# One perceiver block on one core: ternary weights transposed by DMA, rounds 1 and 2 in another order, scores ahead of the weighted sum in odd rounds, and the last codes in halves

## The reference

```python
def xattn(Q, K, Wq_d, W_qk, Wkv_d, Wv_u):          # 16 heads of 32
    C_q, C_kv = Q @ Wq_d, K @ Wkv_d                # 512 -> 64, 512 -> 32
    CqWqk = (C_q @ W_qk).reshape(b, n, 16, 32)
    scores = einsum('bnhl,bkl->bhnk', CqWqk, C_kv) / sqrt(32)
    attn = softmax(scores)
    V_up = (C_kv @ Wv_u).reshape(b, nkv, 16, 32)
    return einsum('bhnk,bkhd->bnhd', attn, V_up).reshape(b, n, 512)
def attn(x, Wqkv, bqkv, Wo, bo):                   # one head of 128
    q, k, v = split(x @ Wqkv + bqkv)
    return softmax(q @ k.T / sqrt(128)) @ v @ Wo + bo
def ffn(x, weight, hadamard):
    xh = x @ hadamard
    s = max(max|xh| over the row, 1e-5) / 7
    xq = clip(round(xh / s), -8, 7) * s            # 4-bit codes
    scale = max(mean|weight| over a row, 1e-5)
    wq = where(weight/scale > .5, 1, where(weight/scale < -.5, -1, 0)) * scale
    return xq @ wq.T
x = x + xattn(layernorm(x), ctx, ...)
x = x + attn(layernorm(x), ...)
x = x + ffn(layernorm(x), weight, hadamard)
```

## Time and profile before

| | |
|---|---|
| median of 3 runs | 314.23 us (314.06 to 314.25) |
| profiled execution | 315.06 us |
| its span | 313.3 us |
| TensorE busy | 299.5 us, 96% |
| VectorE busy | 246.9 us, 79% |
| ScalarE busy | 208.1 us, 66% |
| GpSimd busy | 90.0 us, 29% |
| DMA, share of 16 engines | 26.1% |
| chain that ended last | PE 74%, DVE 11%, ACT 6%, DMA 3% |

### The profile page before, as it was taken

How to read it: one execution, slowest core, us unless ns; L and a number is a source line. 1 busy time by engine, 2 the same in 40 slices (tenths; PEclk the granted TensorE clock), 3 DMA queues, 4 the chain that set the end, 5 groups by cost and what they waited for, 6 DMA issues and landing times.

```text
span 313.3 us, 8324 instructions
## 1 busy us (share of the span) xinstructions
PE 299.5 (96%) x3043; PEld 207.5 (66%) x3058; DVE 246.9 (79%) x530; ACT 208.1 (66%) x587; POOL 90.0 (29%) x130
## 2 busy tenths in 40 slices
PE   7997989999999999999999999999999999999993
PEld 6754857667576766768576766768576866648642
DVE  1689798887879878887879878887879878896366
ACT  2578478768596676768596676768596777784400
POOL 2008304140323324051323324051323324141411
PEclk9999799999999999999999999999999999999998
DMA  7995002051311603041310603051311102000001
GB/s 216 376 363 187 4 8 96 19 189 31 106 49 36 186 1 134 17 157 61 108 43 33 184 0 134 17 173 44 110 43 63 26 0 69 19 35 2 33 0 67
DMA packets 20968, 26.94 MB, mean 86 GB/s; under 512 B 10704, under 2 KB 11472, under 8 KB 20944
## 3 DMA queue, kind: packets, MB, share of 16 engines
q1 hardware_dynamic: 20944, 26.62, 26.1%
HBM read 20.71 MB, written 4.19 MB: 80 GB/s over the span
## 4 chain that ended last, share of the span: by engine, by line
PE 74%; DVE 11%; ACT 6%; DMA 3%; SPq 2%; issue 2%; POOL 0%; DVEq 0%; POOLq 0%
PE ps L1009 10%; PE ps L1074 9%; PE ps L957 7%; PE ps L1132 5%; PE ps L1112 4%; PE ps L1078 4%; PE ps L1162 4%; ACT prob L385 4%; PE ps L967 3%; PE ps L1185 3%; PE ps L1156 3%; DMA bo_row<-bo 3%; PE ps L1046 3%; PE ps L1030 2%; DVE mx L614 2%
## 5 line engine op out<-in xcount | busy, mean ns | idle before, releaser
L385 ACT ACTIVATE prob<-ps,nmx,qk_scale 128x128 f32<-128x128 f32 x240 | 89.8, 469 | 34.9 <-DVE nmx L618 34.9
L1009 PE MATMUL ps<-had_s,x3t 128*128 128x512 f32 x104 | 48.2, 605 | 0.7 <-ACT x3t L379 0.7
L614 DVE TENSOR_REDUCE mx<-ps 128x8 f32<-128x1024 f32 x31 | 37.7, 1217 | 7.0 <-PE ps L1132 7.0
L334 POOL TENSOR_TENSOR qk_scale<-aux,power 128x1 f32<-128x1 f32 x16 | 9.3, 580 | 98.4 <-DVE aux L636 98.4
L623 DVE TENSOR_REDUCE sum_a<-prob 128x8 f32<-128x1024 f32 x30 | 35.8, 1210 | 0.0
L379 ACT ACTIVATE prob_t<-ps 128x512 f32<-128x512 f32 x63 | 34.8, 622 | 0.7 <-PE ps L957 0.3
L1009 PEld LDWEIGHTS ps<-had_s,x3t 128*128 128x128 f32 x104 | 18.6, 190 | 24.5 <-issue 22.7
L957 PE MATMUL ps<-ident,prob 128*128 128x128 f32 x240 | 31.8, 276 | 2.1 <-ACT prob L385 2.1
L957 PEld LDWEIGHTS ps<-ident,prob 128*128 128x128 f32 x240 | 26.6, 141 | 5.5 <-ACT prob L385 4.7
L1074 PE MATMUL ps<-x2t,wqkv_s 128*128 128x128 f32 x224 | 28.6, 281 | 0.4
L1074 PEld LDWEIGHTS ps<-x2t,wqkv_s 128*128 128x128 f32 x224 | 26.1, 192 | 2.2 <-ACT x2t L379 1.3
(11 more groups left out here) (200 smaller groups left out, 577.1 us busy)
## 6 DMA issues: line engine op xcount, KB each, us to landing
ct<-ctx_cols SPq DMA_DIRECT2D x16, 512.0 KB, 4.8
xt<-x_cols SPq DMA_DIRECT2D x16, 256.0 KB, 2.9
xr<-x_rows SPq DMA_DIRECT2D x16, 256.0 KB, 4.2
y<-res SPq DMA_DIRECT2D x15, 256.0 KB, 2.0
had_s<-hadamard SPq DMA_DIRECT2D x1, 1024.0 KB, 7.7
w_rows<-weight SPq DMA_DIRECT2D x1, 1024.0 KB, 10.7
wqkv_s<-wqkv SPq DMA_DIRECT2D x1, 768.0 KB, 8.4
wqk<-w_qk SPq DMA_DIRECT2D x2, 128.0 KB, 4.3
```

What stands on the lines that cost most here:

```text
L385: last = nc.scalar.activation(prob[:, h, :], ps[:, h // 4, (h % 4) * P:(h % 4) * P + P], ACT.Exp, bias=nmx[:, h:h + 1], scale=qk_scale[:])
L614: V.tensor_reduce(mx[:, h], ps[:, 2 * half:2 * half + 2, :].rearrange("p r (c k) -> p (r c) k", c=EC), AX.X, ALU.max).then_inc(done["mx"], 1)
L1009: mm = pe.matmul(ps[:, B4, :], x3t[:, c, :], had_s[:, c, :], start=(c == 0), stop=(c == EC - 1))
```

## The change

1. **Ternary weights.** The 16 transposes on TensorE (L946) and the two copies on ScalarE go. In their place SP's queue issues four DMA transposes of a block of 128 x 512 bf16 each, two in round 1 and two in round 2, these behind the DMAs of the codes of pair 0. TensorE waits for all four before the first integer product.
2. **Rounds 1 and 2.** ScalarE copies the latents of round 1 behind all 16 exponentials. `weight_sizes(3)` moves out of round 0 into round 1. `ternary(1)` stands in front of `second_max` in round 1, `ternary(2)` in round 2 in front of amax. Six more constant products stand in front of `transposed(2)` in round 1, and three more near the start of the program.
3. **Scores first in odd rounds** (from round 3 on): TensorE makes ckv in front of s2, and the scores in front of p2's transpose and the weighted sum. VectorE copies ckv (`context`) in place of ScalarE, has the row variance in front of the q_t copy, and makes both halves of the maxima at the end of the odd round; the next, even, round has none of its own at its start.
4. **The end.** The integers of pair 13 stand in front of the transposes of x2n, with one constant product in place of three. The codes of pair 15 are made, transposed and clipped in two halves of 256 columns.

The diff, cut to its core:

```diff
+        def scores_first(i, par):
+            return par == 1 and not (isinstance(i, int) and i <= 1)
...
+            def ternary_by_dma(c):
+                sp.wait_ge(tern_done, c + 1)
+                sp.dma_start(tern_t[:, :, c * P:(c + 1) * P], tern[:, c, :], transpose=True).then_inc(ternary_turned, 16)
...
                 if quant and (not pre or i < PAIRS - 1):
                     codes_by_dma(i - 2)
+                if pre and 1 <= i <= 2:
+                    for c in range(2):
+                        ternary_by_dma(2 * i - 2 + c)
...
-                if front and not (isinstance(i, int) and i == 0):
+                if front and not (isinstance(i, int) and 0 <= i <= 1):
                     latents()
-                if isinstance(i, int) and i == 2:
-                    ternary_copy(0, B1)
...
                     exps(11, 16).then_inc(done["exp"], 1)
+                    if isinstance(i, int) and i == 1:
+                        latents()
...
-                if front and not (isinstance(i, int) and i == 0):
+                if front and not scores_first(i, par) and not (isinstance(i, int) and i == 0):
                     after(act, made["ckv"], i + 1)
                     copy(ckv[:, 1 - par], ps[:, B1, 0:2 * SKV]).then_inc(read["ckv"], 1)
...
+                def context():
+                    after(dve, made["ckv"], i + 1)
+                    V.tensor_copy(ckv[:, 1 - par], ps[:, B1, 0:2 * SKV]).then_inc(read["ckv"], 1)
...
-                if cross and not (first and i == 1):
+                if cross and (par == 1 or first and i <= 2) and not (first and i == 1):
                     largest(i, 1)
...
                     ternary(0)
                     sums(1)
                     second_query()
+                    ternary(1)
                     second_max()
                     row_variance()
                     row_scale()
-                    ternary(1)
-                    ternary(2)
...
+                    if first and i == 2:
+                        ternary(2)
                     after(dve, made["had"], i - 2)
                     V.tensor_reduce(amax[:], ps[:, B4, :], ...)
...
                     largest(i + 1, 0)
+                    if scores_first(i, par):
+                        largest(i + 1, 1)
...
                 if first and i == 1:
+                    keep_busy(6, B3)
                     transposed(2)
                     transposed(3)
...
+                if front and scores_first(i, par):
+                    after(pe, read["qk"], i - 1)
+                    after(pe, read["lat"], i + 1)
+                    projected()
...
-                if cross:
+                if cross and not scores_first(i, par):
                     weighted_sum()
+                if front and scores_first(i, par):
+                    scores()
                 if self_:
                     after(pe, done["exp2"], i - 1, 2)
                     pe.transpose(ps[:, B3, 0:P], p2[:], ident[:]).then_inc(made["p2t"], 1)
+                if cross and scores_first(i, par):
+                    weighted_sum()
...
                 if quant:
+                    if first and i == 2:
+                        pe.wait_ge(ternary_turned, 16 * EC)
                     after(pe, read["qit"], i - 2)
...
+            quantizer(N, 3, amax_n, floor3_n, step_n, qinv_n)
+            after(dve, made["qit"], 1)
+            for h in range(2):
+                cols = slice(h * E // 2, (h + 1) * E // 2)
+                V.tensor_scalar(z[:, cols], ps[:, 3, cols], qinv_n[:], ROUND, ALU.mult, ALU.add).then_inc(half_z, 1)
+                dve.wait_ge(half_z, h + 1)
+                V.tensor_scalar(qi[:, cols], z[:, cols], ROUND, QMAX, ALU.subtract, ALU.min).then_inc(half_codes, 1)
...
             second_scores(N - 1, B3)
-            keep_busy(3, B1)
-            x2_turned(N, 2)
             after(pe, read["qit"], N - 2)
             for c in range(EC):
                 mm = pe.matmul(ps[:, B4, :], qi_t[:, c, :], tern_t[:, c, :], start=(c == 0), stop=(c == EC - 1))
             mm.then_inc(made["int"], 1)
+            keep_busy(1, B1)
+            x2_turned(N, 2)
```

More of the change, by code:

```diff
@@ L740, in body @@
                     sums(1)
-                if front and not (first and 0 <= i <= 1):
+                if front and not scores_first(i, par) and not (first and 0 <= i <= 1):
                     row_variance()
@@ L1098, in body @@
                     mm.then_inc(made["s2"], 1)
-                if front and not (first and i == 0):
+                if front and not scores_first(i, par) and not (first and i == 0):
                     projected()
@@ L1118, in scores @@
                 def scores():
-                    if first and i == 2:
-                        pe.wait_ge(ternt_read, 2)
                     if alone(i):
@@ L1293, in _ @@
             keep_busy(5, B1)
-            quantized_turned(N, 2)
-            keep_busy(1, B1)
-            after(pe, read["qit"], N)
+            for h in range(2):
+                pe.wait_ge(half_codes, h + 1)
+                for c in range(2):
+                    mm = pe.transpose(ps[:, (2, B2)[h], :].bitcast(BF16)[:, c * P:(c + 1) * P],
+                                      qi[:, (2 * h + c) * P:(2 * h + c + 1) * P], ident_b[:])
+                mm.then_inc(half_turned, 1)
+                keep_busy(1, B1)
             for h in range(2):
                 for c in range(EC):
+                    if h == 0 and c % 2 == 0:
+                        pe.wait_ge(half_clipped, c // 2 + 1)
                     mm = pe.matmul(ps[:, h, 0:E // 2], qi_t[:, c, :], tern_t[:, c, h * E // 2:(h + 1) * E // 2],
```

52 lines of the change are left out of this document (21 added, 31 removed).

## The result

The changed kernel takes 317.97 us (median of 4 runs, 317.46 to 318.19) against 314.24 for the kernel before beside it; the ratio is 1.0113 (95%: 1.0094 to 1.0132). The forecast was 313.0. The profiled execution took 317.89 us, span 316.1. Part of the 1.1% is the draw: twelve later executions of the changed kernel have a median of 316.56 beside 315.10 for 27 of before, a ratio of 1.006 (1.0034 to 1.0086). The sign holds, the size is about half.

What follows compares the result with a forecast made beforehand. TensorE, busy 96% of the span, was taken as the bound, so only its stalls or low clock count. Terms -1.6 + 0.6 - 0.2 = -1.2 us gave 313.9 us profiled, 313.0 median; range 311.2 to 315.0.

Steps and rivals of the forecast that it cites:

- the last of part 1: Round 2: the last ternary transpose, issued at 56.35, lands at 58.8; TensorE, there at 58.0, waits 0.8 us.
- part 1: Rounds 1 and 2, with ternary transposes moved to DMA: 1.6 us gained in all.
- The bound by which each waits for the one before: Round 2 transposes each wait for the one before to land, 2 x 2.4 after the codes: nothing gained, or 0.8 lost.
- rival D: The new transposes land one after the other, so part 1 gives nothing: +0.4, 314.6 us; chance 10%.
- rival B: No change: the clock falls in round 1 despite the fill, 1.5 of part 1 gone: +0.3, 314.5 us; chance 10%.
- 0.7 to 0.9: Round 2: TensorE's wait in us for the second softmax, at the line called L1142 in the kernel before.
- The 0.4 that VectorE was to give back in round 1: Round 1: `ternary(1)` in front of `second_max` lets L1142 come 1.1 us earlier, not 1.5; ScalarE's ckv copy makes it 1.0.
- 2.4 us gained if they cost no wait: Upper bound of the gain in rounds 1 and 2, if the ternary transposes cost TensorE no wait.
- The port rule: VectorE and GpSimd share a port exclusively: `ternary(2)` or POOL's floor up to 0.6 later, part 1 gives 1.0, sum 313.6.
- Part 2: Scores first in odd rounds: six odd rounds cost 6 x 0.33 = 2.0, less 1.4 of even-round stall: plus 0.6 us.
- Rival A: Slower: VectorE becomes the bound of the odd rounds, ckv copy later and x3 held: +1.3, 315.5 us; chance 18%.
- Part 3: The end: reordered integers of pair 13 and codes in halves give 0.2 us together, bounds 0.5 gained and 0.2 lost.

Runs made afterwards that it cites:

- the three in a row: Kernel with ternary transposes first and no scores first, plus spare DMA transposes nobody reads behind the codes' in rounds 3 and 14; the execution took 312.65 us.
- the filled wait: Changed kernel with seven filler products on TensorE ahead of the wait for the ternary transposes in round 2; 315.48 us.
- the kernel of 312.96 us: Changed kernel with ternary transposes issued ahead of the codes' in round 2 and odd rounds in their order of before; 312.96 us, ratio to before 0.995.
- that of 312.44: Changed kernel with ternary transposes first, no scores first, and the second ternary block behind the second maximum and row variance and scale in round 1; 312.44 us.
- 312.74: Changed kernel with ternary transposes first, odd rounds and end as before, second ternary block late; 312.74 us, ratio to before 0.994.

## Why the prediction was wrong

The sum was made for the profiled execution: 313.9, measured 317.9. By its steps:

- **The step that failed** is the last of part 1: "2.4 us pass from issue to landing", "TensorE would be there at 58.0 and waits 0.8". TensorE was there at 58.87 and waited 1.99. The issue times were right (codes 54.67, last transpose 57.2 for "53.8" and "56.35", both 0.87 late with everything else). The landing was 3.6 us instead of 2.4, with a fetch of instructions among its packets: 1.2 us. The bound by which each waits for the one before (53.8 + 3 x 2.4 = 61.0, "0.8 lost") had the landing right, 60.8, for a wrong reason: the three in a row refute it, and rival D's mechanism with it. As a bound of part 1 it failed, since the head of round 3 came 2.2 us later than before.
- **What was missing** is the price of a wait of that size. Behind the 1.99 us the clock was 0.50 for three microseconds, and L1179 to the head of round 3 took 3.30 us instead of 1.51: 1.8 us. I had weighed the clock for round 1 (rival B) and not for the wait that I myself added, so the sum has this term at nothing. With a forecast of 0.8 idle that looked safe; with the landing at 61.0, my own bound, TensorE would have stood 3 us. The price is not paid each time: six of the 12 later executions have a mean clock of .997 or more and 315.3 to 316.0 us, near the 315.48 of the filled wait, and all four of the first comparison happened to be of the others.
- **The start**: first scores came 2.1 us later than in the profile of before, and 0.87 of it was left in round 2. Round 1 takes 16.86 us after a late start and 17.4 to 17.9 after an early one, so it gives more than half of it back. It belongs to the execution, not to the change: it comes and goes in both kernels. Nor is it an amount to take off, since the changed kernel's execution with the early start took 317.43.
- In the first profile these are 1.2 + 1.8 + 0.87 = 3.9 of the 4.0; the rest is the end, forecast at -0.2 and measured at 0, less 0.1 in the rounds.
- **The rest of part 1 held, but for one term.** Fillers, full clock in round 1, L1161's wait of "0.7 to 0.9" (0.9), all as written. The 0.4 that VectorE was to give back in round 1 for `ternary(1)` is not there: round 1 takes 17.79 us with it in front of `second_max` (the kernel of 312.96 us) and 17.78 with it behind (that of 312.44), where before took 19.23, so round 1 gave 1.4 and not 1.0. With the transposes first and the same start (first scores 10.14), the first integers come at 57.78, where the earlier trace rows has 60.43: 2.65 us gained for the "2.4 us gained if they cost no wait".
- **The port rule** did not bite where it was feared. `ternary(2)`'s L608 took 0.49 us at 48.97, as alone; the rival sum of 313.6 by that rule is not borne out. The next L608, of `ternary(3)` at 50.76, took 1.14 us beside GpSimd's tensor_tensor, and it was not free: VectorE's steps to the codes stand behind it without idle time up to 54.3, when SP's wait ended. The kernel before had nearly the same there (1.01 at 51.31), so it hardly counts in the difference. GpSimd's row in the changed kernel:

```profile
50.34 1.27 POOL L339 TENSOR_TENSOR x2b<-x,const_row 128x512 f32<-128x512 f32 x1
```

- **Part 2** was forecast at +0.6 and measured at +0.49 in the medians and +0.37 in the profiles. The pieces were off in opposite ways: idle before the scores 0.43 for "0.26", 0.18 for the 0.2 at x3, but only at the heads of rounds 4 and 14 and not between the loop's rounds, odd rounds 18.86 for "18.7", even ones 16.42 for "16.6". Rival A (315.5) did not happen; VectorE has 16.56 of 18.86 us and holds only the scores.
- **Part 3**: forecast -0.2, measured 0. The idle time moved: L1225 now waits 0.58 for x2t. **Early fillers**: forecast nothing, measured 313.02 against 312.96.
- **From execution to median** I took 0.83 off as if it were an offset. It was the clock's fall in round 1 in that execution (13 of 27 executions of before have such a mean clock), which the change removes. The kernels without the wait show the true gain, 1.5 us (312.96 against 314.49) to 1.9 (312.74 against 314.63), of which the six fillers alone give 0.75 (313.88 against 314.63). The rest agrees with the transposes gone from TensorE (round 2: 19.10 us with fillers only, 17.82 with both); that part was not run alone.

## What to carry to other kernels

A transfer that is issued from a queue starts when what stands ahead of it in that queue has had its wait, not when its data exist: the two ternary blocks were ready 4.0 and 1.6 us before SP's wait for the codes ended, and two lines in another order were worth 3.7 us between the two profiles and 2.8 between the medians of two runs made beside each other (313.66, and 316.43 with fewer early fillers, which are worth nothing). Where a change adds a wait, price it twice, once for the wait and once for the clock behind it, and take its upper bound for the second: idle times of 0.9 us were free here; 1.7 to 2.9 us cost another 1.3 to 1.8 in the profiles where the clock fell, which was about every second execution. And if one execution is the base of the sum, check whether its mean granted clock is that of the others; a fall of clock in it is part of what can be gained, not an offset.

## What the runs showed of the hardware

- A fetch of instructions (one packet, 0.02 MB, on the instruction queue) among the packets of a transposing DMA made these take 149 to 237 ns each instead of 20, and the last ternary transpose landed after 3.5 to 4.1 us instead of 2.4 in all five profiles that have it behind the codes'. The codes' transposes show it too: in the kernel of 312.96 us the one of round 3, with a fetch at its issue (69.6 us), took SP 2.3 us to issue instead of 1.2 and landed after 3.6, and the slowest of its 13, issued at 105.1 in the loop's first pass with a fetch at 107.6, after 4.5.
- Idle times on TensorE and the clock after them: 0.9 and 1.48 us, full; 1.70, 1.99, 2.08, 2.15, 2.33 and 2.90 us, half for about three to four microseconds (one profile each). The changed kernel's executions of full mean clock were not profiled, so what spared them is open. With the wait filled by products whose result nobody reads, the mean clock was .996 or more in all of the 12 + 12 executions.
- The first scores of the changed kernel started at 12.16 us in one execution and at 10.45 in another, those of the kernel before at 10.06 and 11.79, with the same program. In the late ones TensorE's products took nearly twice as long up to about 10 us (L1018 0.98 us for 0.64), in the early ones only up to 4 to 6 us; what decides it is open.
